# A graph layer stack on one core: single row tiles moved in two pieces of 64 and 61 partitions in place of three of 64, 48 and 13

## The reference

```
xn = layernorm(x)
# graph branch: 53125 edges, two convolutions (g = 1, 2), h0 = xn
m   = h[src] * rel_g[edge_type]                    # gather rows, gather relations
m   = concat(m[:half] @ W_in_g, m[half:] @ W_out_g)
agg = segment_sum(m * (1 / deg)[dst], dst)
h   = h + res * tanh(agg + h @ W_loop_g + b_g)
gnn = h @ mu_w + mu_b                              # after g = 2
# mixing branch: 4 layers of linear attention (8 heads) and a 256-1024-256 feed-forward, over all rows
x = x + gnn + mix(xn)
out = x + ffn(layernorm(x))                        # shared MLP plus top-2 of 4 experts
```

## Time and profile before

| | |
|---|---|
| median of 3 runs | 1943.16 us (1937.86 to 1951.39) |
| the profiled execution, its own time | 1951.01 us |
| its span, first to last instruction | 1949.2 us |
| busy share of PE, DVE, ACT, POOL | 90%, 63%, 32%, 67% |
| mean granted TensorE clock | 0.970 |

### The profile page before, as it was taken

How to read it: one execution, slowest core, us unless ns; L and a number is a source line. 1 busy time by engine, 2 the same in 40 slices (tenths; PEclk the granted TensorE clock), 3 DMA queues, 4 the chain that set the end, 5 groups by cost and what they waited for, 6 DMA issues and landing times. The chain is left out here.

```text
span 1949.2 us, 28362 instructions
## 1 busy us (share of the span) xinstructions
PE 1757.6 (90%) x9423; PEld 1294.2 (66%) x9423; DVE 1223.5 (63%) x3583; ACT 628.7 (32%) x1552; POOL 1300.5 (67%) x1297
## 2 busy tenths in 40 slices
PE   2788999998899999989999978987998998988998
PEld 1355867776587777758777645655776676766787
DVE  6777455664756576575556464487665666478766
ACT  4442233343233434333333332231221222222333
POOL 6776777777777777777777733755777676666300
PEclk9999999999899999999999999999999999999999
DMA  9667666667766666776666764667867565555301
GB/s 250 196 200 234 195 207 192 200 191 224 245 197 207 204 193 202 220 248 196 192 203 209 210 192 127 188 197 215 241 192 214 183 202 184 167 176 179 108 14 27
DMA packets 195923, 371.44 MB, mean 191 GB/s; under 512 B 39343, under 2 KB 127445, under 8 KB 195780
## 3 DMA queue, kind: packets, MB, share of 16 engines
q0 software_dynamic: 74304, 220.71, 39.0%
q1 hardware_dynamic: 93124, 126.68, 20.2%
q10 hardware_dynamic: 28352, 22.24, 4.2%
HBM read 305.39 MB, written 64.95 MB: 190 GB/s over the span
## 5 line engine op out<-in xcount | busy, mean ns | idle before, releaser
L1049 POOL DMA_INDIRECT xg<-h_rows,idx_tab x416 | 426.8, 1026 | 205.9 <-issue 125.1
L1049 POOL DMA_INDIRECT xg<-xn_rows,idx_tab x416 | 432.7, 1040 | 141.6 <-issue 123.4
L1001 POOL DMA_INDIRECT rg<-relation_rows,idx_tab x416 | 417.2, 1003 | 136.4 <-issue 126.2
L2880 PE MATMUL ps_hid<-hT,wff 128*128 128x250 f32 (+1 forms) x1920 | 372.3, 347 | 7.0 <-ACT gT L2314 7.0
L2892 PE MATMUL ps_down<-wff,gT 128*125 128x256 f32 x1600 | 366.1, 382 | 0.0
L2880 PEld LDWEIGHTS ps_hid<-hT,wff 128*128 128x128 f32 x1920 | 313.7, 192 | 59.1 <-issue 27.0
L1144 DVE TENSOR_TENSOR xg<-xg,rg 128x256 f32<-128x256 f32 x832 | 296.6, 418 | 71.4 <-DMA xg<-h_rows,idx_tab 40.1
L2892 PEld LDWEIGHTS ps_down<-wff,gT 128*125 128x125 f32 x1600 | 295.4, 189 | 46.3 <-issue 5.1
L2751 PE MATMUL ps_seg<-xg,hot 128*61 128x257 f32 (+1 forms) x1664 | 233.9, 404 | 39.3 <-DVE xg L1144 34.3
L2314 ACT ACTIVATE gT<-ps_hid,b1p 128x250 f32<-128x250 f32 (+1 forms) x480 | 176.8, 434 | 286.6 <-PE ps_hid L2880 286.4
L2751 PEld LDWEIGHTS ps_seg<-xg,hot 128*61 128x61 f32 (+1 forms) x1664 | 103.1, 139 | 134.6 <-issue 67.3
(11 more groups left out here) (382 smaller groups left out, 2420.5 us busy)
## 6 DMA issues: line engine op xcount, KB each, us to landing
second_relation_rows<-rg SPq DMA_DIRECT2D x104, 512.0 KB, 4.0
rg<-second_relation_rows SPq DMA_DIRECT2D x104, 512.0 KB, 4.0
wff<-L_mix_W ACTq DMA_DIRECT2D x8, 1024.0 KB, 7.2
rg<-relation_rows,idx_tab POOLq DMA_INDIRECT x416
xg<-xn_rows,idx_tab POOLq DMA_INDIRECT x416
xg<-h_rows,idx_tab POOLq DMA_INDIRECT x416
h_rows<-qT_all SPq DMA_DIRECT2D x25, 64.0 KB
qrow<-h_rows ACTq DMA_DIRECT2D x25, 64.0 KB
```

What stands on the lines that cost most here:

```text
L1001: pool.indirect_dma_start(rg[:, k, :], None, rel_d, indices(step, 1)).then_inc(s_edge[k // UNIT], 16)
L1049: pool.indirect_dma_start(xg[:, k, 0:D], None, rows, indices(step, 0)).then_inc(s_edge[k // UNIT], 16)
L2880: ins = pe.matmul(hidden, w1[:, c, ff * P:(ff + 1) * P], hT[:, a:z, c, :], start=c == 0, stop=c == KC - 1)
```

## The change

A second list, TILE_PIECES, is set to STRIPS = ((0, 64), (64, 125)). `move_tile` goes through it, and every wait and start value that counts the landings of single tiles counts 16 * 2 in place of 16 * 3. `move_group` keeps the three pieces.

```diff
@@ -171,6 +171,7 @@
     PIECES = ((0, 64), (64, CUT), (CUT, T))
+    TILE_PIECES = STRIPS
@@ -490,7 +491,7 @@
-        s_h1 = [counted(f"h1_stored{k}", 16 * len(PIECES)) for k in range(SLOTS)]
+        s_h1 = [counted(f"h1_stored{k}", 16 * len(TILE_PIECES)) for k in range(SLOTS)]
@@ -624,6 +625,7 @@
         MOVED = 16 * len(PIECES)
+        TILE_MOVED = 16 * len(TILE_PIECES)
@@ -783,7 +785,7 @@
         def move_tile(eng, rows, dram, t, done, store=False):
-            for a, z in PIECES:
+            for a, z in TILE_PIECES:
                 ends = rows[a:z], tile_rows(dram, t, a, z)
                 eng.dma_start(*(ends[::-1] if store else ends)).then_inc(done, 16)
@@ -948,7 +950,7 @@
-            sp.wait_ge(s_out, MOVED * (NG - 1 + GT))
+            sp.wait_ge(s_out, MOVED * (NG - 1) + TILE_MOVED * GT)
@@ -1827,7 +1829,7 @@
-                    dve.wait_ge(s_h1[t % SLOTS], MOVED * (t // SLOTS) + MOVED)
+                    dve.wait_ge(s_h1[t % SLOTS], TILE_MOVED * (t // SLOTS) + TILE_MOVED)
@@ -3223,7 +3225,7 @@
-                        pe.wait_ge(s_hx[h], (t - h) // AHEAD * MOVED + MOVED)
+                        pe.wait_ge(s_hx[h], (t - h) // AHEAD * TILE_MOVED + TILE_MOVED)
```

More of the change, by code:

```diff
@@ L914, in _ @@
             for k in range(SLOTS):
-                sp.wait_ge(s_h1[k], MOVED * (len(range(k, NT, SLOTS)) + 1))
+                sp.wait_ge(s_h1[k], TILE_MOVED * (len(range(k, NT, SLOTS)) + 1))
             def load_relations(u):
@@ L1038, in _ @@
                     for k in range(SLOTS):
-                        pool.wait_ge(s_h1[k], MOVED * (len(range(k, NT, SLOTS)) + 1))
+                        pool.wait_ge(s_h1[k], TILE_MOVED * (len(range(k, NT, SLOTS)) + 1))
                 for step in range(STEPS2):
@@ L2473, in joint @@
                     for k in range(SLOTS):
-                        act.wait_ge(s_h1[k], MOVED * (len(range(k, NT, SLOTS)) + 1))
+                        act.wait_ge(s_h1[k], TILE_MOVED * (len(range(k, NT, SLOTS)) + 1))
                     for t in range(GT):
@@ L3269, in turn_sums @@
                     h = t % GT
-                    pe.wait_ge(s_hx[h], (dense_loads(h) + t // GT + 1) * MOVED)
+                    pe.wait_ge(s_hx[h], (dense_loads(h) + t // GT + 1) * TILE_MOVED)
                     turned = transpose_rows(pe, ps_x2[:, KC * T:2 * KC * T], qrow[:, h, :])
```

## The result

The changed kernel takes 2022.27 us (median of 4 runs, 2019.65 to 2027.69), the kernel before 1944.07 us in the runs beside it. The ratio is 1.040, with a 95% interval of 1.036 to 1.045: slower by 78 us. The profiled execution has a span of 2025.9 us against 1949.2, that is 76.7 us more.

What follows compares the result with a forecast made beforehand. PE, busy 90% of the span, was taken to bound most of it, SP and the stores' round trip the dense stage. Terms 60 + 6 + 15 + 3 + 2 = +86 us on 1943.2 gave 2029 us, range 1980 to 2078.

Steps and rivals of the forecast that it cites:

- The 61 rows run on one engine: Single-tile loads and stores: each 61-row piece, 61 being prime, runs in series on one DMA engine, first pieces on 16.
- Rival (a): Tile loads and stores: the 61 rows spread over many engines, so spared issues make it faster, 1923 us; chance 7%.
- Price of a row, 44 ns: Rows in series on the one engine: each takes 44 ns, a little under double 23.5 ns; bounds 40 and 57.
- Dense stage, loads and stores together: Dense stage, 19 tiles with loads and stores: the one engine sets 6.96 us a tile against 3.81, +60 us.
- Last six tiles: End of the dense stage, stores without loads: 3.7 us a tile in place of 2.7, +6 us.
- ACT's run: ACT's consecutive load issues: its queue fills for the shared engine and PE idles longer, 0 to +25, taken as +15 us.
- Gathers beside ACT's loads: 1350 to 1829 us: gathers falling into ACT's load bursts land up to 2.5 us late, 0 to +10, taken as +3.
- The end: Very last tile's store: 61 rows on one engine, 2.6 us more less 0.5 us of an issue, uncovered, +2 us.
- Nothing is caught up later: After the dense stage: PE is full again from 1202 us on, so the whole delay counts on the path.
- Rival (b): Dense stage slows on one engine but later stages absorb it, leaving some 15 us, 1958 us; chance 4%.
- Rival (c): One engine and worse: rows at 57 ns and more, ACT stands 30 us, gathers cost 15, 2090 us; chance 10%.
- What would be seen: Dense stage signs: DVE's store wait rises from 28.8 to about 90 us, PE's busy share falls from 0.79 to about 0.5.

## Why the prediction was right

Its claim was 2029 us, in 1980 to 2078; measured were 2022. The mechanism is the forecast one, and the parts run alone add up to nearly the whole: 59 for the dense stage, 15 for ACT's loads and 1 for the end, of 78 us. The total is closer than the largest term, which is some luck: the dense stage was put 13 us too high, the other terms together 4 us too low. Step by step, with the trace's parts of the 76.7 us against its +86:

- *The 61 rows run on one engine.* Shown: the floor of 25 GB/s, and the runs with 59 and with 60 rows. Rival (a), that the rows are spread, is refuted for loads and for stores, and with it the 1923 us of the coalescing rule (the Trainium skill, "DMA: Bandwidth & Descriptors", "Rules for kernel authors") in this case; with the rows of the loads spread, two pieces brought 0.998. The Trainium skill's rule on the number of engines (same page, "Why a DMA increments its semaphore by 16 and not by 1") agrees with all runs: 61 and 59 on one, 60 on 15. That stores behave as loads had been carried over from a single load of 103 rows; the run with the stores alone shows it. The queue's packets in the dense stage, without the relation stores, fell from 172 to 141 a tile, where 170 and 142 had been counted.
- *Price of a row, 44 ns.* It was 41 ns (25 GB/s) in the dense stage, and 42 ns for the stores at the end. The even beat in the earlier trace rows and its doubling had put an upper end to it and the true value lay below. The mean over the busy queue, 46 ns a packet and 57 ns a row, was too high for a row in series. Other queues are not the reason: with 59 rows, 1225 to 1235 us, where nearly all packets are of this queue, it is 47 ns a packet too (477 packets, 14.0% of 16 engines). What makes packets longer in the peaks is open.
- *Dense stage, loads and stores together: +60 for 19 tiles.* +46.8 for 18, 49 for 19. The pace was 6.41 and not 6.96 us. 138.4 rows at 41 ns are 5.7 us, which leaves 0.7 us a tile for the gathers where 0.87 was taken; their queue's busy share there, 12.7% of 115.3 us, is 0.81 us a tile. This is the term that was too large, by its two prices and not by its mechanism: that the engine and not the round trip sets the pace is shown by the four buffers (6.32 us), and that neither loads nor stores alone fill it by the two single runs (4.49 and 4.64 us).
- *Last six tiles: +6.* +8.4, from store 18 on, which is seven stores: 1.2 us each where 1.0 had been put.
- *The first six loads: 0, with up to +5.* +2.0 up to store 0.
- *ACT's run: +15.* +14.0, and +15 when timed alone. 255 rows in 24 us are 94 ns a row, about half of the engine, as assumed; but the 255 rest on the queue's limit of some 110 rows, which only the earlier trace rows shows. That ACT is held back by a full queue had been read off SP's start; here the ten issues take 19 to 20 us in every run with 61 rows, and the fifteen of before 7 to 9 us.
- *Gathers beside ACT's loads: +3.* +3.1 from ACT's table load to the last DVE instruction. It was only seen as a sum; no run takes it apart. In that stretch DVE's wait for the reload of x, L1319, is 14.3 us against 2.6 before, which may hold part of it.
- *The end: +2.* +2.5 in the profile, not measurable in time.
- *The upper bound, +130.* Its parts add up to +132 (94 + 6 + 5 + 15 + 10 + 2). Nothing hangs on it.
- *Nothing is caught up later.* From SP's first relation load to ACT's run the two traces differ by 0.1 us in 131.7. Rival (b) is refuted. Rival (c), 2090 us, isn't met: its price of 57 ns a row and its 30 us at ACT were both too high.
- *What would be seen.* The wait at L1833 was 80.6 and not about 90 us. PE's busy share in the stage fell to 0.62 and not to 0.5, for a reason of its own (below).

## What to carry to other kernels

These transfers cost what their busiest DMA engine had to do. Before merging pieces, look at how the row count divides: here 60 rows lay spread and 59 or 61 in series, and one row in the count is worth 79 us. The sign was a DMA view with an even floor of 24 or 25 GB/s between peaks, and the stretch with less total traffic (a DMA share of 0.33 in place of 0.60, below) was the one bound by DMA. Look also at long runs of issues on a compute engine's queue: with one DMA engine behind, ACT stood for 24 us in place of 10, and its own work with it. And a wait that looks like the bound may only be the next in line: a fourth buffer gained 0.6% with spread rows and nothing with the rows on one engine.

## What the hardware showed beside this

PE did the same work in more time. The windows of the kernel before (the first row) and of the changed one (the second), from store 0 to store 18, with PE's busy us and instructions first and the granted clock, DMA share and GB/s last:

```profile
1115.00:1184.00 69.00, 54.61 (x358) 33.13 (x354) 39.42 (x100) 19.93 (x40) 20.41 (x22) 0.98 0.60 172
```

```profile
1117.00:1233.00 116.00, 71.86 (x353) 42.79 (x350) 39.82 (x98) 19.96 (x40) 19.02 (x20) 0.75 0.33 99
```

Standing between the tiles, for up to 7.1 us at a time, PE was granted 0.75 of its clock in place of 0.98, a mean of stretches at 2.4 GHz (1.00 from 1117 to 1127 us) and at 1.2 GHz (0.50 from 1147 to 1157 us), and its 353 matmuls took 204 ns each where 358 took 153. It should have cost little while the DMA engine was the bound, but no run separates that. In the last six tiles it is no part of the 8.4 us: the granted clock is 0.82 before (1184 to 1203 us) and 0.81 after (1233 to 1260 us), and a matmul takes 209 and 208 ns. The share of busy time, 0.79 before and 0.62 after, therefore understates how idle PE had become.
